# Inverse square roots of two layer norms computed on GpSimd instead of VectorE

## What is computed

```python
def _layernorm(x, eps=1e-05):
    m = jnp.mean(x, axis=-1, keepdims=True)
    v = jnp.var(x, axis=-1, keepdims=True)
    return (x - m) / jnp.sqrt(v + eps)

x = L0_attn_hidden_states                        # (8, 1024, 256)
# attention: 16 heads of 16, rope on the last 256 positions, softmax(q k^T / 4) v, out projection
x = x + _L0_attn_ref(_layernorm(x), ...)
# feed-forward: 16 experts of width 512, each takes its 128 best tokens of each batch; one shared expert
x = x + _L0_ffn_ref(_layernorm(x), ...)
```

## Time and profile before

| | us |
|---|---|
| median of 3 runs | 2423.66 |
| lowest and highest run | 2422.8, 2426.49 |
| span of the profiled execution | 2427.3 |
| attention, from the first maxima of batch 0 to the last | about 1398 of it |

### The profile page before, as it was taken

The page is one execution under the profiler, slowest core; times in us unless marked ns, Lnnn a source line. Parts: engine busy times, 40 slices in busy tenths (PEclk is TensorE's granted clock), DMA queues, the critical chain, the costliest instruction groups (busy, mean ns, idle before and its releaser), DMA issues. The chain is left out here.

```text
span 2427.3 us, 44076 instructions
## 1 busy us (share of the span) xinstructions
PE 2283.2 (94%) x16398; PEld 1340.3 (55%) x16398; DVE 1891.8 (78%) x3506; ACT 1632.3 (67%) x3168; POOL 886.1 (37%) x1223
## 2 busy tenths in 40 slices
PE   5899999999999999999999988899997999999996
PEld 4233334334334334334333323788886888888886
DVE  5999999999999999999999994466654555555553
ACT  2599999999999999999999987323323343333432
POOL 4051451451451451441542220000003666666664
PEclk8799999999999999999999999799998999999998
DMA  2000011010010010010010010332322545454443
GB/s 76 1 18 1 1 36 36 1 50 22 1 55 17 9 61 3 19 53 1 19 36 1 19 36 18 126 100 78 104 61 81 115 109 112 87 112 113 100 99 35
DMA packets 104364, 122.74 MB, mean 51 GB/s; under 512 B 7553, under 2 KB 91393, under 8 KB 104193
## 3 DMA queue, kind: packets, MB, share of 16 engines
q1 hardware_dynamic: 79616, 86.90, 11.2%
q0 software_dynamic: 24576, 33.57, 8.1%
HBM read 78.50 MB, written 41.94 MB: 50 GB/s over the span
## 5 line engine op out<-in xcount | busy, mean ns | idle before, releaser
L474 DVE TENSOR_REDUCE sb_MX<-ring 128x1 f32<-128x512 f32 x2048 | 1284.5, 681 | 82.0 <-PE ring L782 65.4
L606 ACT ACTIVATE sb_PR<-rot 128x512 f32<-128x512 f32 x2048 | 1123.3, 621 | 102.8 <-PE rot L793 92.3
L782 PE MATMUL ring<-sb_KT,sb_QT 32*128 32x512 bf16 x2048 | 517.1, 390 | 48.9 <-DVE sb_MX L474 36.5
L804 PE MATMUL pv<-sb_PR,sb_VA 128*32 128x512 f32 x4096 | 547.0, 606 | 2.9 <-ACT sb_OT L661 0.6
L782 PEld LDWEIGHTS ring<-sb_KT,sb_QT 32*128 32x128 bf16 x2048 | 128.1, 91 | 632.9 <-DVE sb_MX L474 565.8
L793 PE MATMUL rot<-sb_QT,sb_KT 32*128 32x512 bf16 x2048 | 422.1, 386 | 1.6
L1095 ACT ACTIVATE ex_GL<-ex_gu 128x512 f32<-128x512 f32 x128 | 76.4, 597 | 347.4 <-PE ex_gu L63 345.2
L1162 DVE TENSOR_TENSOR ex_HF<-ex_GL,ex_gu 128x512 f32<-128x512 f32 x128 | 87.5, 684 | 250.8 <-ACT ex_GL L1095 250.8
L1059 POOL DMA_INDIRECT out<-ex_YS,ex_rows_out x128 | 208.8, 1631 | 44.3 <-issue 43.8
L1016 POOL TENSOR_TENSOR ex_pool_scratch<-identity 128x1 f32<-128x1 f32 x96 | 35.1, 366 | 477.6 <-POOLq L859 332.0
L61 PE MATMUL ex_gu<-ex_XH,weights_high 128*128 128x512 f32 x512 | 200.4, 391 | 2.4 <-DVE ex_XL L1154 2.4
(11 more groups left out here) (168 smaller groups left out, 4272.2 us busy)
## 6 DMA issues: line engine op xcount, KB each, us to landing
sb_XA<-x SPq DMA_DIRECT2D x8, 1024.0 KB, 5.5
sb_XR<-x SPq DMA_DIRECT2D x8, 1024.0 KB, 5.8
out<-sb_XR SPq DMA_DIRECT2D x8, 1024.0 KB, 4.5
xn<-sb_XN SPq DMA_DIRECT2D x8, 1024.0 KB, 4.5
sh_XG<-xn SPq DMA_DIRECT2D x16, 512.0 KB, 5.5
sh_X<-out SPq DMA_DIRECT2D x16, 512.0 KB, 4.9
weights<-WgT SPq DMA_DIRECT2D x16, 512.0 KB, 4.0
weights<-WuT SPq DMA_DIRECT2D x16, 512.0 KB, 5.6
```

Of the source, the lines that this page charges most:

```text
L474: nc.vector.reduce_max(MX[:, unit % 2, half, j, qt % 4:qt % 4 + 1], ring[m % RING][:], AX.X).then_inc(ring_done, 1)
L606: out = nc.scalar.activation(PR[V % P_STEPS][:, j, :], R[:], ACT.Exp, scale=0.25)
L782: nc.tensor.matmul(ring[m % RING][:], QT[g][r, P * qt:P * qt + P], KT[g][r, 512 * half:512 * half + 512], start=True, stop=True, tile_posi ...
L804: out = nc.tensor.matmul(pv_bank[head(j), :], VA[b % 2][:, kt, 4 * g + j, :], PR[V % P_STEPS][:, j, :], start=(kt == 0), stop=(kt == TT - 1))
```

## The change

The 14 inverse square roots within the steps leave DVE. POOL gets `inverse_root`: add eps, raise to the power -0.5, and one Newton step of four instructions, each waiting for the one before it. It stands in POOL's list at S = 7 and S = 27. `mv_ready`, raised by the last merging instruction of DVE, tells POOL that the variance is there. The first and the last inverse square root (before batch 0's steps and behind batch 7's) stay on DVE.

```diff
+        minus_half = sb("minus_half", [P, TT], F32)
+        spread = sb("spread", [P, TT], F32)
+        refine = sb("refine", [P, TT], F32)
...
+        mv_ready = [sem(f"mv_ready{n}") for n in range(2)]
...
             own = Tally(pool_own)
+            own.inc(nc.gpsimd.memset(minus_half[:], -0.5))
...
+            def inverse_root(n, count):
+
+                y = rstd[n]
+                pool.wait_ge(mv_ready[n], count)
+                own.inc(nc.gpsimd.tensor_scalar(spread[:], mv[n][:, :, 1], EPS, None, ALU.add))
+                own.wait(pool)
+                own.inc(nc.gpsimd.tensor_tensor(y[:], spread[:], minus_half[:], ALU.pow))
+                own.wait(pool)
+                own.inc(nc.gpsimd.tensor_tensor(refine[:], y[:], y[:], ALU.mult))
+                own.wait(pool)
+                own.inc(nc.gpsimd.tensor_tensor(refine[:], refine[:], spread[:], ALU.mult))
+                own.wait(pool)
+                own.inc(nc.gpsimd.tensor_scalar(refine[:], refine[:], -0.5, 1.5, ALU.mult, ALU.add))
+                own.wait(pool)
+                nc.gpsimd.tensor_tensor(y[:], y[:], refine[:], ALU.mult).then_inc(rstd_ready[n], 1)
...
+                if more and S == 7:
+                    inverse_root(0, b + 1)
+                if b and S == 27:
+                    inverse_root(1, b)
...
-            def merge_stats(n, tiles):
+            def merge_stats(n, tiles, last=False):
...
-                    own.inc(nc.vector.bn_aggr(mv[n][:, i, :], stats[:, i, :]))
+                    step = nc.vector.bn_aggr(mv[n][:, i, :], stats[:, i, :])
+                    if last and i == tiles[-1]:
+                        step.then_inc(mv_ready[n], 1)
+                    else:
+                        own.inc(step)
...
-                if more and 7 <= S <= 12:
-                    newton(0, 2 * (S - 7))
-                if prev and 26 <= S <= 31:
-                    newton(1, 2 * (S - 26))
...
-                    merge_stats(0, range(4 * (S - 4), 4 * (S - 3)))
-                if more and 7 <= S <= 12:
-                    newton(0, 2 * (S - 7) + 1)
+                    merge_stats(0, range(4 * (S - 4), 4 * (S - 3)), S == 5)
...
-                    merge_stats(1, range(TT))
-                if prev and 26 <= S <= 31:
-                    newton(1, 2 * (S - 26) + 1)
+                    merge_stats(1, range(TT), True)
```

## The result

The changed kernel takes 2409.5 us (median of 4 runs, 2406.89 to 2412.7) against 2425.07 us (4 runs, 2422.8 to 2426.91) for the kernel before: ratio 0.9933, 95% interval 0.9919 to 0.9947. It is faster by 0.7%. The forecast was 2408.6 us, with a range of 2403 to 2419 us. The profiled span is 2410.8 us against 2427.3 us. The difference lies in attention. In the table, all values are from the profiles and in us; a step begins with its first maximum on DVE. The forecast for one batch is worked out from the prediction's terms: 179.29 - 2.46 + 0.1 us.

The account below looks back on a forecast made before the run. Neither DVE nor ACT alone was taken to bound attention; each step lasts as long as whichever has more in it. 14.8 + 1.0 - 0.7 = 15.1 us off 2423.66 us gave 2408.6 us, range 2403 to 2419 us.

Parts of the forecast that it names:

- The stretches argument: Attention steps 7 to 12 and 26 to 31: batches 1 to 6 lose 1.04 and 1.42 us each, 14.8 us in all.
- The second term: Steps 26 to 31: 17.15 us against 15.73 us in batch 0, so 1.42 us gained in each of batches 1 to 6.
- Holding, not instruction count: DVE in the steps: being held by POOL costs 2.4 us per batch; the 1.8 us of plain cost shows nearly nothing.
- The two single chains: First inverse square root of batch 0, second of batch 7: 0 to 0.9 us each, taken as 0.5, so 1.0 us.
- The power: POOL's raising to -0.5 in the new chain, in no earlier row: taken as 1 us, chain about 2.7 us, costing nothing.
- the cover: POOL's idle time and slack before PE reads its results at S = 27; gone at a power of some 5 us.
- The join at S = 27: DVE's `join_halves`, two SBUF inputs, held by the chain's last instructions: 0.1 us, seven times, a loss of 0.7 us.
- The slow-power rival: Power of Y us holds DVE's join at S = 27, costing 7 x (Y - 1.2) us; at 5 us 2434 us; chance 0.12.
- The chance of 0.08 for slower: Part of the slow power's 0.12 chance, left after 0.04 for ending within 0.2%.
- ACT takes it all back: Rival in attention: stretches shorten, but ACT, 92% busy, falls behind and batches end as before, 2423 us; chance 0.08.
- The total: Whole kernel: gain 14.8 + 1.0 - 0.7 = 15.1 us, span 2412.2 us, median 2408.6 us; chance 0.75 for 5 to 20 us.

## Why the prediction was right, point by point

- **The stretches argument** was right. The path's loss was read from batches 7 and 0, which do the same steps without an inverse square root: 1.04 us was measured as 16.76 - 15.72 = 1.04 us, and 1.42 us as 17.15 - 15.46 = 1.69 us, together 2.73 us. The steps around give 0.23 us of it back (37.10 to 37.14 us in steps 13 to 25, 87.90 to 88.09 us in steps 32 to 63 of batch 2, all of the latter in step 32), which leaves 2.50 us. Over batches 1 to 6 the gain is 1075.74 - 1060.76 = 15.0 us, against 14.8 us. The second term was too small because batch 0 was no perfect likeness: its step 26 takes 2.61 us, that of batches 1 to 6 now 2.37 us, and this one step holds nearly all of the 0.27 us by which the term was short. Why step 26 of batch 0 is longer was not looked into.
- **Holding, not instruction count**: shown. Taking the holding away and leaving as many instructions gives 2.37 of 2.50 us per batch; adding one multiplication costs 1.0 us in the batches where it is held and nothing where it is not; a row maximum in its place costs nothing.
- **The two single chains** (first of batch 0, second of batch 7), taken as 1.0 us together: those two stretches are 0.31 us (15.58 to 15.27) and 0.68 us (15.62 to 14.94) shorter, 1.0 us. The sum is right; the even split was not.
- **The power** was taken as 1 us and is 1.67 us. It changed nothing, as the cover is 3.65 us longer than it; the forecast had put its end at a power of some 5 us, and the runs work out to 5.3 us.
- **The join at S = 27**, a loss of 0.7 us, did not happen. Two parts of this step failed: the power is longer than taken, so that the join meets it and not the small instructions behind it, and the power does not hold it.
- **The slow-power rival** rested on that hold and falls with it: by its formula a power of 2.93 us costs 1.7 us a batch, and it costs nothing; even one of 8.06 us leaves the join at 0.17 us. A slow power does end slower than before, but through POOL's own lateness, which costs nothing up to a power of some 5.3 us instead of 1.2 us, and through the clock that falls behind PE's waits. The chance of 0.08 for slower was attached to the wrong mechanism.
- **ACT takes it all back**: no. ACT is busy 15.34 of 15.72 us in the shortened stretch, but the steps around give back only the 0.23 us above. Whether ACT, DVE (15.28 us) or the exchange with PE bounds the stretch now was not tested.
- **The total**: the spans differ by 16.5 us, where 15.1 us were forecast. 15.0 us are in batches 1 to 6 and 1.0 us in the two single chains; the remaining 0.5 us are in steps 0 to 6 of batch 0, which took 20.8 to 21.4 us in kernels that do not differ there, so they are scatter and not the change. The medians differ by 15.6 us. That they meet the forecast of 2408.6 us to 0.9 us is partly luck: the kernel before came out 1.4 us higher (2425.07 against 2423.66 us) than the forecast started from, and the join's 0.7 us were not lost.

## What to carry to other kernels

Look at the longest duration of an instruction beside its median: one far above the median that ends together with a GpSimd instruction is the sign of a hold. Five such meetings cost 2.4 us per batch here, as many instructions without them 0.13 us. Another engine is one cure. Another form in the same slot, the row maximum, gave nearly the same time, but no run computed the inverse square root in such a form; and moving the instruction a slot further only found it other partners. Nor does every hold cost time: the one of 0.30 us at S = 35 cost nothing.

## What the runs showed of the hardware that was not expected

- The power on GpSimd over 8, 16 and 48 columns of 128 partitions takes 1.67, 2.93 and 8.06 us, which fits 0.16 us for each column and 0.4 us ahead of them; a multiplication over 8 takes 0.20 us.
- A multiplication of a 128 x 8 tile on DVE, with two SBUF inputs, is held to its end by GpSimd's 128 x 512 subtraction (1.27 us, started 0.02 us earlier), and not at all by the power, met 0.56 and 0.92 us after its start. The join of the maxima, two SBUF inputs of 128 x 16, is held by a 128 x 512 multiplication at S = 35 (0.47 us) and not by the power, met 1.26 us after its start, nor by the power of 48 columns, met 1.27 and 7.52 us after its start. The Trainium skill, "SBUF — State Buffer", section "Who interferes with whom", says that the first of the two keeps the shared ports for the whole instruction; the subtraction agrees, the power does not. Whether the power holds them in its first half microsecond was not tried, nor why it lets them go; that it reads its few columns at the start and computes after is a guess.
- With recorded starts 0.02 us apart and always in the same order, the hold came in four batches of six in the same run, with 1.0 us at stake each time.
- Waits of PE of 2.1 and 2.8 us were followed by a granted clock of 0.50, which made the next step 1.4 to 1.5 us longer; in batch 1 a wait in the same place was not.
